# High and low parts of W1 and W3 laid word by word in turn in the main weights of a routed SwiGLU layer

## What is computed

```
xn = layernorm(x)
h_t = A * h_{t-1} + (xn_t @ B_w.T + B_b)         # along each sequence, A = sigmoid(log_A)
s = h @ C_w.T + C_b
c = softmax over the top 2 of 8 experts of (xn @ Wr + br), 0 for the others
y_e = (silu(xn @ W1[e]) * (xn @ W3[e])) @ W2[e]  # W1, W3: 256 x 512, W2: 512 x 256, per expert
out = x + s * silu(sum_e c_e * y_e)
```

## Time and profile before

| | |
|---|---|
| median of three runs | 792.95 us (792.79 to 793.4) |
| the profiled execution | 792.44 us |
| its span | 790.7 us |
| PE busy | 765.4 us, 97% |
| PEld busy | 683.5 us, 86% |
| DVE busy | 518.5 us, 66% |
| ACT busy | 376.2 us, 48% |
| POOL busy | 464.8 us, 59% |

### The profile page before, as it was taken

The page is one execution under the profiler, slowest core; times in us unless marked ns, Lnnn a source line. Parts: engine busy times, 40 slices in busy tenths (PEclk is TensorE's granted clock), DMA queues, the critical chain, the costliest instruction groups (busy, mean ns, idle before and its releaser), DMA issues.

```text
span 790.7 us, 17130 instructions
## 1 busy us (share of the span) xinstructions
PE 765.4 (97%) x5399; PEld 683.5 (86%) x5399; DVE 518.5 (66%) x1083; ACT 376.2 (48%) x667; POOL 464.8 (59%) x477
## 2 busy tenths in 40 slices
PE   4999989999999999999999999999999999999997
PEld 2554449999999999999999999999999999998786
DVE  6988975776778657666866664555656765542766
ACT  3985234544455445445544554445546644442530
POOL 4742847687577667845783686468557856554000
PEclk9999999999999999999999999999999999999999
DMA  9999813544565444425643644264537554943994
GB/s 291 336 314 322 138 39 110 136 73 67 134 134 113 100 97 97 67 49 140 141 68 93 167 67 75 42 142 67 112 68 200 97 131 96 330 70 41 315 372 164
DMA packets 101842, 111.02 MB, mean 140 GB/s; under 512 B 15634, under 2 KB 89236, under 8 KB 101748
## 3 DMA queue, kind: packets, MB, share of 16 engines
q0 software_dynamic: 25920, 35.54, 27.3%
q1 hardware_dynamic: 50032, 50.34, 20.2%
q10 hardware_dynamic: 25796, 24.20, 10.7%
HBM read 66.61 MB, written 43.45 MB: 139 GB/s over the span
## 4 chain that ended last, share of the span: by engine, by line
PE 87%; DVE 7%; DMA 2%; issue 2%; ACT 1%; POOL 0%; ACTq 0%; DVEq 0%; POOLq 0%; SPq 0%
PE bank L1538 15%; PE bank L1512 15%; PE bank L1513 15%; PE bank L1514 15%; PE bank L1539 7%; PE bank L1646 6%; PE bank L1412 4%; DVE xnT L1090 2%; PE bank L1500 2%; DVE stats L961 1%; PE bank L1375 1%; PE bank L1564 1%; PE bank L1565 1%; PE bank L1563 1%; PE bank L1642 1%
## 5 line engine op out<-in xcount | busy, mean ns | idle before, releaser
L609 POOL DMA_INDIRECT y_rows<-y_sb,token_at x128 | 214.6, 1677 | 143.1 <-DVE y_sb L1208 73.3
L1512 PE MATMUL bank<-xh,W_sb 128*128 128x256 f32 x1008 | 283.2, 281 | 0.1
L1514 PE MATMUL bank<-xl,W_sb 128*128 128x256 f32 x1008 | 281.8, 280 | 0.0
L1513 PE MATMUL bank<-xh,W_sb 128*128 128x256 f32 x1008 | 281.7, 279 | 0.0
L1512 PEld LDWEIGHTS bank<-xh,W_sb 128*128 128x128 f32 x1008 | 189.2, 188 | 2.3 <-DVE xl L1156 0.4
L1513 PEld LDWEIGHTS bank<-xh,W_sb 128*128 128x128 f32 x1008 | 189.3, 188 | 0.0
L1514 PEld LDWEIGHTS bank<-xl,W_sb 128*128 128x128 f32 x1008 | 189.0, 188 | 0.0
L1538 PE MATMUL bank<-W_sb,hh 128*128 128x512 f32 x512 | 187.7, 405 | 1.0 <-DVE y_sb L1208 0.9
L1196 DVE TENSOR_TENSOR hbuf<-hbuf,bank 128x512 f32<-128x512 f32 x128 | 87.5, 687 | 153.5 <-PE bank L1514 149.0
L600 POOL DMA_INDIRECT xg<-xn_rows,token_at x128 | 144.9, 1132 | 38.3 <-issue 18.6
L1539 PE MATMUL bank<-W_sb,hl 128*128 128x256 f32 x512 | 143.8, 281 | 0.0
(11 more groups left out here) (255 smaller groups left out, 921.7 us busy)
## 6 DMA issues: line engine op xcount, KB each, us to landing
x_late<-L_attn_x SPq DMA_DIRECT2D x24, 512.0 KB, 9.2
raw<-L_ffn_W ACTq DMA_DIRECT2D x24, 512.0 KB, 4.3
odd_raw<-L_ffn_W ACTq DMA_DIRECT2D x21, 512.0 KB
xn_rows<-h_sb SPq DMA_DIRECT2D x16, 512.0 KB, 6.5
y_rows<-xnT SPq DMA_DIRECT2D x4, 2048.0 KB, 15.7
yy<-y_rows SPq DMA_DIRECT2D x16, 512.0 KB, 9.3
out<-x_late SPq DMA_DIRECT2D x11, 512.0 KB, 6.6
x_kept<-L_attn_x SPq DMA_DIRECT2D x4, 512.0 KB, 6.8
```

The lines of the kernel that those rows point to most:

```text
L609: return eng.indirect_dma_start(out=y_rows, out_offset=rows, in_=y, in_offset=None, bounds_check=T + TW - 1, oob_is_err=True, compute_op=A ...
L1512: eng.matmul(part, high, x_h, start=k == 0, stop=False)
L1513: eng.matmul(part, low, x_h, start=False, stop=False)
L1514: last = eng.matmul(part, high, x_l, start=False, stop=k == KD - 1)
```

## The change

The high and low parts of W1 and W3 in `W_sb` take turns word by word: word 2c is the high part and word 2c + 1 the low part of column c. `w_part` returns these views for n = 0 and 1 of `W_sb`, so ScalarE's copy writes with a step of two words, and VectorE's subtraction reads one operand and writes with that step. `product` reads its stationary tiles with a step of two words. W2, the odd tiles' weights, all moving operands, the count of instructions, their order, their waits and the size of the tensors are as before. On every engine the row of instructions is the same, one for one.

```
@@ -325,9 +325,15 @@
+        def in_pairs(at, cols, low):
+
+            return W_sb[:, 2 * at:2 * (at + cols)].rearrange("p (c s) -> p c s", s=2)[:, :, low]
+
         def w_part(n, low, of=W_sb):
 
             at, cols = W_PARTS[n]
+            if n < 2 and of is W_sb:
+                return in_pairs(at, cols, low)
             if n == 2:
                 return of[:, 2 * at:2 * (at + cols)].rearrange("p (k s d) -> p k s d", k=KI, s=2)[:, :, low, :]
             return of[:, low * LO_AT + at:low * LO_AT + at + cols]
@@ -1507,7 +1513,7 @@
                     part = o[m // 2][:, m % 2 * TW:(m % 2 + 1) * TW]
                     for k in range(KD):
                         at = w_at + k * I + m * P
-                        high, low = W_sb[:, at:at + P], W_sb[:, LO_AT + at:LO_AT + at + P]
+                        high, low = in_pairs(at, P, 0), in_pairs(at, P, 1)
                         x_h, x_l = high_x[:, k * TW:(k + 1) * TW], low_x[:, k * TW:(k + 1) * TW]
                         eng.matmul(part, high, x_h, start=k == 0, stop=False)
                         eng.matmul(part, low, x_h, start=False, stop=False)
```

## The result

Slower by 0.85%: the ratio of after to before is 1.0085, with a 95% interval of 1.0067 to 1.0103. The medians are 798.37 us (797.77 to 799.85, four runs) and 792.87 us (791.45 to 793.4, four runs), 5.5 us apart. The profiled execution took 797.77 us, with a span of 796.0. The likeliest case of the prediction, no change, did not come true; a small form of rival A did.

What follows compares the result with a forecast made beforehand. TensorE, busy 97% of the span, was taken as the bound, its W1 and W3 matmuls paced by moving columns. Loads, ScalarE's writes and VectorE's subtractions summed to 0 + 0 + 0, giving 793.0 us, range 790.5 to 806.

Steps and rivals of the forecast that it cites:

- rival A: Stepped loads exposed at every W1 and W3 matmul: 41 us at a quarter more, 283 us if doubled; chance 0.16.
- no change: Whole kernel: time stays within 0.2%, 1.6 us, of the forecast 793.0 us; chance 0.66.
- rival B: VectorE's low-part subtractions for W1 and W3 slow by their stepped write: up to 12.5 us, time 805.5; chance 0.14.
- The bound: TensorE, 97% busy: W1 and W3 matmuls 118 ns apart, paced by moving columns at 0.46 ns each, not by loads.
- Step 1: TensorE's 3,072 W1 and W3 loads at a step of two words: cost 0, upper end 283 us.
- The room: Slack of a load behind its W1 or W3 matmul: 13 ns, since 105 of 118 ns are used.
- step 3: VectorE's low-part subtractions for W1 and W3: d, the extra time of each, 0; upper end 1.28 us.
- Step 2: ScalarE's high-part writes for W1 and W3: at most 0.24 us more each, hidden in a 0.61 us gap, cost 0.
- C: W1 and W3 matmuls become faster, starts under 0.115 us apart: up to 34 us less, 759; chance 0.04.
- D: The change does nothing that an engine notices; this is the forecast itself, chance 0.66.
- the list at its end: Signs to check: product starts still 0.12 us apart, load records still 188 ns, write times and up-product starts as forecast.

Runs made afterwards that it cites:

- steps 3 and 4: Kernel before with W1 and W3 loads at a step of three or four words inside their own part: 964.0 and 1143.43 us against 790.87.
- e4: Kernel before with W1 and W3 products cut to 128 of 256 moving columns and their loads at a step of two words: 806.49 us.
- experiment 2: Kernel before with W1 and W3 moving columns halved, one run with dense loads (781.88 us), one with loads at a step of two words (806.49 us).
- e1: Changed kernel with its interleaved writes kept but TensorE's loads dense again: 792.23 us, ratio 0.9999 to the kernel before.
- e7: Kernel before with the down product's stationary tiles read at a step of two words: 791.03 us against 790.87.
- e8: Kernel before with a step of two words on the W1 and W3 loads of the low parts only: 794.01 us against 790.87.
- Step 8: Kernel before with W1 and W3 loads at a step of eight words inside their own part: 1167.45 us against 792.17.
- e11: Kernel before with the down product's stationary tiles read at a step of four words: 850.38 us against 792.17.

## Why the prediction was right or wrong, point by point

**The range held by luck.** 798.37 us lie between 790.5 and 806, but the room above the forecast was put there for all of rival B, VectorE's writes, which came to nothing. Rival A was said to stay out of it, but was priced only at 41 and 283 us, so its small form lay inside. What was forecast with the highest chance, no change beyond 0.2%, failed, and one step failed in it, the first.

**The bound** was read rightly: TensorE's distance of 118 ns set by the moving columns, with the down product as the control. It stayed at 235 and 118 ns while the others moved.

**Step 1, the loads, failed in one term.** The sentence is "Middle: only the fetch path halves its speed, 2 x 57 = 114 ns, which is under 118 and costs nothing". That the step would act on the fetch was right, and steps 3 and 4 show the time growing with the blocks fetched. But the term measured 118 to 119 ns (e4) and not 114, and its source, 57 ns from 140 less 83, is borne out by no run: those loads start 82 ns apart or more. The edge was 4 ns away and the term 4 to 5 ns short, so that "nothing" became 2 ns on 3,072 matmuls, the 6.1 to 6.8 us of which the stage's 6.5 are made. The rule "under 118 costs nothing" is itself only good to 1 or 2 ns here: the load's single distances scatter by some 3 ns about their middle, which by the estimate of experiment 2 makes 1.3 ns. A term worked out from two durations, to be compared with something 4% away, should have been given as a range across the edge.

**The room was mis-sized too.** "105 of 118 ns is used: 13 ns" came from subtracting two latencies. With the columns halved the dense load keeps 112 ns: 6 ns of room. Rival A had the right mechanism and place, but by this room it put its point of decision at a load record above 201 ns, and the record came to 198; and its cheapest priced case was 131 ns, 41 us (3,072 x 13 ns is 40). Between the forecast at 114 and that case lay the real one.

**Rival B and step 3** are settled as forecast: d = 0. 1,222 ns against 1,225 for a write and one read at a step of two. The rule of the Trainium skill on adjacent pairs in VectorE ("Vector Engine (DVE) Microarchitecture Reference", 5.2) would have made that 2.6 us, an estimate from its figure for longer steps, and the trace does not show it at this step. One reading of this step was wrong without effect: the 0.15 us between hl and up at a tight change, read as room for 2d, is the lag behind hl of a TensorE that already waits (0.15 us from matmul to matmul there for 0.118), so there was no room at all.

**Step 2**: ScalarE's write grew by 82 ns on 1,024 words, 0.08 ns a word, for an upper end of 0.24 us, and stayed under its cover; with e1 at 0.9999 the cost on the end is none.

**Rivals C and D.** C fell: no distance got shorter. D, that no engine notices, is the forecast; it fell by the 10 ns in the load record, the first sign that the list at its end asked for.

**Open.** The last 1 to 2 ns: a stepped load beside 256 columns gives 118 in e7, 121 in e8 and 120 in after, where the slower of the two paces gives 118 to 119. Step 8's 240 for 233. Why the down product's loads show the cost in one of two distances only (e11) is explained by how the records are drawn, not shown by a run of its own.

Neither these runs nor the counts point to a layout under before: 118 ns is the columns' pace, and a step of these sizes adds blocks to one stream or the other.

## What to carry to other kernels

Where loads of a stationary tile and moving columns run side by side without gaps, the distance is close to the slower of the two, and 1 to 2 ns over it here where they were equal. So count the blocks of 16 bytes that each one touches in a partition (some 1.8 ns each here, and no less than 112 ns for a load of these products) and compare them before an access gets a step. Measure the room between the two by halving the columns in one run; taking latencies from durations gave twice the room that there was. Compare short differences between runs of equal granted clock: here it moved whole runs of before by 1.6 us (792.9 against 791.25), a quarter of the effect. Where a term ends within a few per cent of the edge that hides it, forecast a small cost times the count, here 2 ns by 3,072, rather than nothing.

## What the runs showed that was not expected

- The cost of a step on TensorE follows the 16-byte blocks touched, and so saturates: 119, 174, 233 and 240 ns for a load at steps of 2, 3, 4 and 8 words. Each step above two was run once.
- A step of two words costs nearly nothing in a stationary operand (112 to 119 ns), and in a moving operand of the same type it takes 118 ns to 227.
- A write with a step of two words costs ScalarE 0.08 ns a word and VectorE nothing that its records show (4 ns at most on 1,024 words).
- A matmul that waits for its load carries the wait inside its own record (e11: 523 ns for 405), with its start 194 ns ahead of the end of the load's record where 72 is usual.
